# A graph layer on one core: the node biases added on GpSimd two tiles at a time in the node stage, not one tile at a time in the stage of keys and values

## The reference, cut to what matters

```python
xn = layernorm(x)
# GNN: gates from the edge attributes, messages summed at their target
gate = sigmoid(silu(rbf @ W1 + b1) @ W2 + b2)
aggr = segment_sum(gate * xn[src], dst)
upd  = silu(concat([xn, aggr]) @ U1 + c1) @ U2 + c2
# attention without softmax, 4 heads
k, v = layernorm_heads(xn @ wk.T), layernorm_heads(xn @ wv.T)
mix  = (xn @ wq.T) @ (k.T @ v / 3125) @ wo.T + bo
x    = x + xn + upd + mix
x    = x + experts(layernorm(x))      # top 2 of 16
```

## Time and profile before

| | before |
|---|---|
| median of 3 runs | 1086.65 us |
| profiled execution, its own time | 1086.7 us |
| its span in the profile | 1084.7 us |
| granted TensorE clock, mean share of full | 0.989 |
| PE busy | 1042.7 us (96%) |
| DVE busy | 886.8 us (82%) |
| POOL busy | 748.9 us (69%) |
| ACT busy | 696.9 us (64%) |

### The profile page before, as it was taken

The page is one execution under the profiler, slowest core; times in us unless marked ns, Lnnn a source line. Parts: engine busy times, 40 slices in busy tenths (PEclk is TensorE's granted clock), DMA queues, the critical chain, the costliest instruction groups (busy, mean ns, idle before and its releaser), DMA issues.

```text
span 1084.7 us, 23741 instructions
## 1 busy us (share of the span) xinstructions
PE 1042.7 (96%) x7960; PEld 983.1 (91%) x7960; DVE 886.8 (82%) x1495; ACT 696.9 (64%) x1091; POOL 748.9 (69%) x705
## 2 busy tenths in 40 slices
PE   5998999999999999999999998999899999999995
PEld 2556899999999999999999998998699999999995
DVE  7997988888999888889888883488687777777773
ACT  4765667766666666666666644656277777777763
POOL 5475777777777777777777766540357777777765
PEclk9999999999999999999999999999999999999998
DMA  7212445444444544444454420226278989889961
GB/s 254 76 54 70 140 141 147 142 143 139 139 144 142 146 142 142 137 141 145 142 145 143 141 80 22 79 69 192 52 218 223 239 218 235 218 231 222 233 189 15
DMA packets 118528, 159.75 MB, mean 147 GB/s; under 512 B 20568, under 2 KB 91052, under 8 KB 118444
## 3 DMA queue, kind: packets, MB, share of 16 engines
q1 hardware_dynamic: 86780, 91.60, 26.1%
q0 software_dynamic: 31104, 66.28, 26.1%
q10 hardware_dynamic: 560, 0.79, 0.2%
HBM read 142.42 MB, written 18.17 MB: 148 GB/s over the span
## 4 chain that ended last, share of the span: by engine, by line
PE 86%; DVE 8%; issue 2%; ACT 1%; DMA 1%; POOL 0%; DVEq 0%; POOLq 0%; ACTq 0%; PEldq 0%
PE ps L1748 25%; PE ps L1955 16%; PE ps L1759 16%; PE ps L1700 8%; PE ps L1967 8%; PE ps L1801 4%; PE ps L1813 2%; PE ps L1826 2%; PE ps L1675 1%; PE ps L1935 1%; DVE st L1090 1%; PE ps L1840 1%; DVE ssq L1107 1%; PE ps L1881 1%; PE ps L1684 1%
## 5 line engine op out<-in xcount | busy, mean ns | idle before, releaser
L1748 PE MATMUL ps<-fr 128*128 128x256 f32 x2352 | 305.6, 286 | 0.8 <-DVE fr L1152 0.5
L1748 PEld LDWEIGHTS ps<-fr 128*128 128x128 f32 x2352 | 288.2, 191 | 1.7 <-DVE fr L1152 1.6
L644 POOL DMA_INDIRECT big<-xn_rows,srcs x200 | 218.7, 1093 | 61.2 <-issue 61.2
L644 POOL DMA_INDIRECT hgx<-xn_rows,srcs x192 | 210.1, 1094 | 58.5 <-issue 58.5
L826 ACT ACTIVATE h1f<-ps,b 128x512 f32<-128x512 f32 x196 | 124.1, 684 | 170.6 <-PE ps L1700 169.4
L1759 PEld LDWEIGHTS ps<-oh,big 128*128 128x128 f32 x1568 | 191.2, 193 | 8.6 <-DVE big L1299 0.5
L1955 PE MATMUL ps<-fr 128*128 128x256 f32 x1536 | 190.5, 283 | 1.5 <-issue 1.3
L1759 PE MATMUL ps<-oh,big 128*128 128x96 f32 x1568 | 189.7, 274 | 0.4 <-DVE big L1308 0.4
L1955 PEld LDWEIGHTS ps<-fr 128*128 128x128 f32 x1536 | 186.8, 192 | 2.3 <-issue 2.1
L1152 DVE TENSOR_TENSOR fr<-h1f,fr 128x1024 fp32r<-128x1024 f32 x98 | 120.5, 1229 | 48.4 <-ACT fr L829 48.3
L719 POOL DMA_INDIRECT out<-xnT,idx x60 | 113.3, 1889 | 41.6 <-issue 34.7
(11 more groups left out here) (246 smaller groups left out, 1421.1 us busy)
## 6 DMA issues: line engine op xcount, KB each, us to landing
big<-in_w SPq DMA_DIRECT2D x128, 256.0 KB, 4.3
rbf<-in_rbf SPq DMA_DIRECT2D x98, 256.0 KB, 3.0
big<-in_w SPq DMA_DIRECT2D x32, 512.0 KB, 4.4
xn_rows<-xn SPq DMA_DIRECT2D x26, 128.0 KB, 2.4
big<-xn_rows,srcs POOLq DMA_INDIRECT x200, 3.1
xn_rows<-hgx SPq DMA_DIRECT2D x24, 128.0 KB, 2.4
hgx<-xn_rows,srcs POOLq DMA_INDIRECT x192, 3.2
out<-x_nodes SPq DMA_DIRECT2D x6, 512.0 KB
```

Of the source, the lines that this page charges most:

```text
L644: pool.indirect_dma_start(hg[i % HB][:, s, :], None, xn_d[:, :], bass.IndirectOffsetOnAxis(srcs[:, col:col + 1], 0))\
L1748: last = mm(ps[:, 2 + 4 * p + s // 2, (s % 2) * D:(s % 2 + 1) * D], h1s[p][a][:, c, s * P:(s + 1) * P], W2s[b][:, c, :], start=c == 0 and ...
```

## The change

GpSimd no longer adds the biases in the stage of keys and values. The sum of the two bias vectors is kept in a tile of its own (`bias`), since `cb` is written over later; three scratch tiles of DVE shrink to make room. The additions take two tiles an operation, 13 in all. Three stand between the last gather and the node stage's first operation, two in each turn of the node loop, and the last two right behind the loop. DVE's `x1(v)` waits for its own pair's addition.

```diff
-BIASAT = {t: (2 * t - 6, min(2 * t - 4, NT)) for t in range(3, 16)}
...
+        bias = sb("bias", [P, D])
...
-        v_a = sb("v_a", [P, NT * 8])
+        v_a = sb("v_a", [P, NT])
...
-            def add_biases(t):
-                pool.wait_ge(s_xn, t + 1)
-                pool.tensor_tensor(x[:, t, :], x[:, t, :], cb[:, 0, :], ALU.add).then_inc(s_xcb, 1)
...
-            link(pool.tensor_tensor(cb[:, 0, :], cb[:, 0, :], cb[:, 1, :], ALU.add))
+            link(pool.tensor_tensor(bias[:, :], cb[:, 0, :], cb[:, 1, :], ALU.add))
...
-                for u in range(*BIASAT.get(t, (0, 0))):
-                    add_biases(u)
...
+            def add_biases(v, n=2):
+                pool.wait_ge(s_xn, NT)
+                xr = x[:, ds(v * 2, n), :]
+                pool.tensor_tensor(xr, xr, bias[:, :].unsqueeze(1).to_broadcast([P, n, D]), ALU.add).then_inc(s_xcb, 1)
             pool.sem_inc(s_slo, 2)
+            for v in range(3):
+                add_biases(v)
...
             with pool.Fori(0, NB // 2 - 2) as j:
                 silu_low(j * 2 + 1, 1)
                 node_low(j * 2 + 3, 1)
+                add_biases(j * 2 + 3)
                 silu_low(j * 2 + 2, 0)
                 node_low(j * 2 + 4, 0)
+                add_biases(j * 2 + 4)
+            add_biases(NB - 2)
+            add_biases(NB - 1, 1)
             silu_low(NB - 4, 1)
             node_low(NB - 2, 1)
...
-            dve.wait_ge(s_xcb, NT)
             def x1(v, q, n):
                 dve.wait_ge(s_uo, v + 3)
+                dve.wait_ge(s_xcb, v + 1)
```

More of the change, by code:

```diff
@@ L166, in gps_layer @@
         rstd = sb("rstd", [P, NT])
-        v_a = sb("v_a", [P, NT * 8])
-        v_b = sb("v_b", [P, NT * 8])
-        v_c = sb("v_c", [P, NT * 8])
+        v_a = sb("v_a", [P, NT])
+        v_b = sb("v_b", [P, NT])
+        v_c = sb("v_c", [P, NT])
         ssq = sb("ssq", [P, NT * 8])
```

## The result

The changed kernel takes 1097.3 us (median of 4 runs, 1096.31 to 1098.46); the kernel before, beside it, 1086.33 (1085.94 to 1088.88). The ratio is 1.0089, 95% interval 1.0074 to 1.0103. Each ratio in this document compares only executions in the faster of the chip's two states. The forecast of 1090.0 was 7.3 us short, and the time is outside its range. The profiled execution took 1096.31 us (span 1094.3).

The account below looks back on a forecast made before the run. TensorE was taken as the bound (busy 96%, 86% of the chain), so GpSimd edits count only through its waits. Terms -2.3 + 0.4 + 2.5 + 2.8 = +3.4 us on 1086.7 gave 1090.0 us, range 1086.6 to 1092.6.

Parts of the forecast that it names:

- Part 1: Keys and values: without additions there, both TensorE waits for DVE's scaled keys go; -2.3 us, bounds -2.6 and -1.0.
- Part 2: End of the edge stage: three additions behind the last gather make DVE's one-hot and message 0.4 late; +0.4 us.
- one DVE message: Behind the last gather: one DVE operation gets through between the three additions, which end at about 648.5 us.
- The bound of +1.8: Behind the last gather: upper bound if additions start only at about 646.5 and meet both one-hot and message.
- Parts 3 and 4: Node stage: product M of pair 4 begins late, +2.5 us; DVE delayed from pair 8 to 11, +2.8 us.
- gets through only when that one GpSimd operation ends: Small DVE operations begun beside GpSimd work: each waits for one GpSimd operation, 1.23 us for a 4-number operation.
- the 0.74 of slack: Node stage, kernel before: product M of pair 4 begins 0.74 us after the `x1(2)` it waits for.
- Rival 3: Cascade: longer additions, a late start behind the last gather, or halved clock after TensorE's stall; 1093.4 us, chance 0.14.
- Rival 1: Node stage: additions give way to DVE's small operations, so only the keys-and-values gain remains; 1084.4 us, chance 0.10.
- the slower side: Whole kernel: a time of 1089.9 us or more, chance 0.48.

Follow-up runs that it names:

- Another run: Against the changed kernel: only the first three pairs' additions stay behind the last gather, the other ten stand in the edge stage; ratio to the kernel before 1.0525.
- the changed kernel's second trace: The changed kernel itself, unedited, run again beside other kernels where the edge stage was longer; ratio to the kernel before 1.006.
- three additions staying: Against the changed kernel: additions of pairs 3, 4 and 5 keep their node-stage places, the others move to the edge stage; ratio to the kernel before 1.0641.
- the last three additions alone: Against the changed kernel: only the last three pairs' additions stay in the node stage, the other ten move to the edge stage; ratio to the kernel before 0.9959.
- the two kernels of the last group: Against the changed kernel: first three additions moved behind GpSimd's first two node-stage low parts, 1092.04 us; the other ten also moved, into GpSimd's pauses, 1083.06 us.
- the kernel with three in the edges: Against the changed kernel: first three pairs' additions moved into the edge stage, behind gathers of groups 20, 45 and 70; ratio to the kernel before 1.0116.

## Why the prediction was wrong

**Part 1 (-2.3): right in kind, mis-sized.** It is -3.5. Both waits up to 80 us are gone, as forecast, and behind 80 us came the 0.3 to 0.4 that the bound allowed (four waits of 2.3 us before, two of 1.9 now). What was mis-sized is the stretch between: I took the two waits by their idle time, 2.3 us, and TensorE was 3.1 us ahead by tile 13. From tile 3 to 5 it gained 1.7 us where the wait was 1.41, from 5 to 7 1.1 where it was 0.92.

**Part 2 (+0.4): the step that failed, and the largest of the errors.** It is +3.9, 2.5 of it hold and 1.4 clock. In the span the changed kernel lost 9.6 us where the sum had 3.4, and 3.5 of the 6.2 missing are here. The working let "one DVE message" through between three additions, and met the one-hot and the message of the last window. It had passed over the one-hot ahead of these (643.24), which begins 0.5 us ahead of the gather's end, and nothing got through: that one-hot was held for all three additions, and the last one-hot came 2.5 us late. Another run shows the same hold of a whole unbroken run (4.49 us over an addition and two low parts), and taking the three away gives 3.8 us back, 1.4 of it clock. It is not so in every execution: in the changed kernel's second trace the additions met no such one-hot, and the first product M came 7.5 us behind the last one-hot, as before. The bound of +1.8 was too low for the same reason: it was counted in operations of GpSimd, not in the length of its queue.

**Parts 3 and 4 (+2.5, +2.8): right** in place and chain, and nearly in size. TensorE's stall is 2.85, and with three additions staying at full clock `x1(7)` comes 3.1 late against `x1(1)`; pairs 8 to 11 lose 3.0, the last three additions alone 2.95. For part 3 the heading "the addition" was too narrow, though its working had two: three additions share the 3.5 us, one alone costs 1.3, of which the 0.74 of slack takes more than half (TensorE waited 0.65). And "gets through only when that one GpSimd operation ends" does not hold for L1082, held over two.

**The clock: a term that the sum didn't have.** The stalls and the gain add up to 5.1 us (-3.5 + 2.5 + 3.1 + 3.0). The rest of the 9.6 us in the span goes with stretches at 0.5: 1.4 in the window sums, 1.3 up to `x1(1)`, 1.4 behind the stall of pair 4, 0.5 after `x1(11)`, where the stretch is 10.2 us for 6.8. Rival 3 named it, at 0.14, but its sum has no term for it. That these are the clock is shown for the one behind pair 4 (4.41, 5.78 and 7.03 us with 0, some 3.4 and some 6.8 us of half clock), for the window sums (3.90 and 5.41) and for the way to `x1(1)` (16.2, 17.5 and 18.8 us, at 1.00, 0.78 and 0.57 over the first 7 us). That the additions brought them is another matter. For the 0.5 after `x1(11)` they did not: the stretch was 10.2 us without any. For the 1.3 it is open: the way to `x1(1)` took 17.7 in the two kernels of the last group, without three additions behind the last gather, but 18.5 in the kernel with three in the edges, and 16.2 in the second trace of the changed kernel. Since the stretch does not follow every stall, the stall of 2.9 us cost 3.1, 4.5 or 5.7 us by `x1(7)`.

**Rival 1's mechanism** (the additions give way) is refuted by the changed kernel's trace: no addition there was given way (1.36 us at most), and each of the operations above was held. The Trainium skill's rule drawn on in the prediction ("SBUF — State Buffer", "Who interferes with whom") agrees as far as the loser waits in full. The section also says that whoever issues first keeps the port pair. By the profile's start times the runs differ: the one-hot began 0.54 us ahead of the additions and lost to all three, and in ten meetings in the edge stages of other kernels an operation of 128x1024 begun 0.25 to 0.46 us ahead of an addition ended 1.1 us behind it. Begun 0.78 to 0.96 us ahead, such operations got through in 1.22 to 1.24 us in all six meetings, and the addition took longer (1.43 to 1.56, the half-size one 0.87).

The time fell on the slower side, which had 0.48; the range ended at 1092.6, as the upper half of rival 3 was left out of it.

## What to carry to other kernels

Where an operation of GpSimd is cheap by its own queue, ask which VectorE operation it holds and who waits for that: the same thirteen additions gave -0.3% or +0.9%, and over +5% with ten to twelve of them in a stage whose gathers ran without slack. Don't queue several GpSimd operations behind one another beside a VectorE operation on the path; put them where VectorE reads PSUM or waits. A stall of TensorE can cost more than its length, so give it a price with the half clock behind it and one without.

## What the hardware showed that I had not expected

- A VectorE operation of two SBUF inputs can be held over several GpSimd operations in a row: 4.71 us over three additions, 4.49 over parts of three operations. In the long chains of small operations VectorE got one through per GpSimd operation (1.15 to 1.28). L1082 there is between the two: held over the rest of a low half and a whole addition (1.93). What separates them wasn't found: the first two began right behind a wait of VectorE (0.16 and 2.96 us), L1082 did not.
- Beside an addition of 1.3 us, operations reading PSUM (128x1024, 1.22 us) kept their length in all the meetings in the edge stage; those of two SBUF inputs ended 1.1 (128x1024), 0.57 (64x512) and 0.43 us (128x384) behind it.
- Where the kernel before takes 1088.8 us, the gathers of the edge stage had two regimes in four kernels: 1.09 to 1.11 us a gather, and, from the first addition placed among them on, 1.25 to 1.26, which adds 0.73 us to every group of four until the end of the stage. Why, and whether it is so everywhere, is open.
- After TensorE's stall of 2.9 us the granted clock was full in one trace, at 0.5 for some 3.4 us in four and for about twice that in two. The same kernel can have either: the changed kernel's two traces differ in two other stretches.
